# Moving one step of a gate's first layer, a residual and a variance bank in a two-block convolution kernel

## The chip, the cores and the metric

One Trainium2 chip, one of its cores. The metric is the device time of one execution in microseconds (us), taken as the median of several runs.

## What is computed

The input is `x` of shape (8, 64, 32, 32). Two blocks follow one another.

The first is a window attention block over channels: layer norm, attention in 8x8 windows with 8 heads and a relative bias, a projection and a residual, then layer norm, an MLP with GELU (64 to 256 to 64) and a second residual.

The second block, cut to what matters here:

```
h     = pw1 @ x + b                       # 1x1 convolution, 64 -> 64
score = sigmoid(fc2 @ relu(fc1 @ mean(h)))     # one per image and channel
mask  = the 32 largest scores of each image
off   = tanh(off_w @ mean(relu(h)))            # 3 x 2 per image
for ksz in (3, 5, 7):                          # depthwise, 32 channels
    w = base[ksz] * (1 + sigmoid(off[i, 0])) + tanh(off[i, 1])
    y[ksz] = dwconv(relu(h) * mask, w)
out = pw @ concat(y) + b + x
```

So each image has its own convolution weights, and they depend on the means of all its pixels. The chain from the means to the weights of an image is called its gate here.

## The kernel before, in words

Two images lie beside each other on the 128 partitions (`bh` is 0 or 1, 64 channels each), and four such pairs (`b4` is 0 to 3) follow in the free dimension: 4096 columns, worked on in 8 chunks of 512 columns (`NG` is 8).

**Attention.** A software pipeline over the 8 chunks: in the step of chunk g TensorE also does work of chunks g+1, g+2 and g-1. The second layer norm of a chunk is `centered2` (mean away), `variance2` (mean of squares), `inverse_deviation2` on ScalarE (Ln, then Exp), and `normalise2` on VectorE.

**MLP and pointwise stage.** For each chunk n: `mlp1(n)` makes four blocks of hidden values in PSUM banks 3 to 6, ScalarE's `gelu` empties them, `mlp2(n)` contracts them into bank 1, VectorE's `add_mlp(n)` adds them to x, `pointwise1(n)` makes h in bank 7 (even n) or 2 (odd n), ScalarE's `relu(n)` writes it into padded images, VectorE's `pool_image(n)` sums it, and GpSimd's `low_image(n)` makes its low part. The last chunk's second layer norm is still under way when this stage begins, so `variance2(7)` stands between `mlp2(1)` and `pointwise1(0)`. ScalarE loads the table for Ln and Exp ahead of `inverse_deviation2(7)` and the GELU table behind it.

**Gates.** Three gates: gate 0 for the pair b4=0, gate 1 for b4=1, gate 2 for b4=2 and 3. Each runs through `gate_means` (VectorE, then two matmuls on TensorE), `gate_hidden` (VectorE), `gate_scores` (TensorE, VectorE), `gate_spread` (VectorE, then two matmuls on TensorE), `gate_mask` and `gate_taps` (VectorE), and then for each image `products`, `add_products` (together `whole_weights`, VectorE) make the fp32 weights. Those are split into a high and a low part: ScalarE's `even_high` and `odd_row_weights` make the high part, VectorE's `low_even` and `low_odd` the low one.

**Convolution.** For each image, a unit (b4, bh): SP copies the padded image, shifted by 0 to 3 rows, onto the four groups of 32 partitions (`copy_images`, four transfers), and TensorE runs 14 tiles of taps. `high_passes` is 14 x 2 matmuls (high weights by high and low image), `low_passes` is 14 matmuls (low weights by high image): 42 matmuls of 512 columns per unit, 8 units. The matmuls of a unit add up in bank 3 + bh. VectorE's `result(b4, bh)` adds bias and residual, and SP stores the image. SP copies the images of the pair b4+1 once the unit (b4, bh) has ended.

**What sets the order.** Every engine's queue is written out by hand; each step waits on semaphores of the others. TensorE's order from the last MLP chunk on is: `pointwise1(5)`, `gate_means(1)`, `mlp2(6)`, `pointwise1(6)`, `gate_scores(1)`, `mlp2(7)`, then the units, with `gate_spread(1)`, `pointwise1(7)`, `gate_means(2)`, `gate_scores(2)` and `gate_spread(2)` put between passes. The lines of this part: L713 layer norm matmuls, L928 `mlp1`, L940 `mlp2`, L950 `pointwise1`, L956/L957 `gate_means`, L963 `gate_scores`, L970/L971 `gate_spread`, L1014 all convolution passes; VectorE L1155 `add_mlp`, L1229 `pool_image`, L1259 `gate_hidden`, L1265 `gate_scores`, L1275 to L1282 `gate_spread`, L1326 to L1337 `whole_weights`, L285 a low part, L1362 `result`; ScalarE L629 `gelu`, L638/L639 `relu`, L560/L564 Ln and Exp, L656/L271/L273 high weights; GpSimd L456 `low_image`; SP L382 `copy_images`, L386 store.

Of the kernel before, what the change touches and what calls it, by code (L numbers as in the profile page):

```python
# [12 lines left out]
NG = COLS // G  # L13
# [5 lines left out]
TAP = 7  # L19
# [7 lines left out]
NKT = (TAP + 1) // SHIFTS * TAP  # L27
# [71 lines left out]
def conv_seq_kernel(nc, d, out):  # L99
# [4 lines left out]
    with ctx:  # L104
# [116 lines left out]

        psum = ctx.enter_context(nc.psum_tensor("psum", [128, 8, 512], F32))
        NORM, MISC0, MISC1, MAX0, PROB0, PV = 0, 1, 2, 3, 5, 7
        VAR2_LAST = 6

        S = {n: sem(n) for n in (
            "zeroed", "k_heads_zeroed", "v_zeroed", "eps_set", "center_in", "consts_in", "x_first", "x_in0", "x_in1", "x_in2", "x_in3", "qkv_in", "raw_in", "weights_in", "rel_in",
# [10 lines left out]
        HIDDEN0, MLP, PW1, GATE, CONV0 = 3, 1, (7, 2), 0, 3  # L238
# [14 lines left out]
        def taps_window(w, m):  # L253

            o = (TAP - KERNELS[m]) // 2
            return w.rearrange("p (h x) o -> p h x o", x=TAP)[:, :, o:TAP - o, :]
# [26 lines left out]
        def low_part(engine, whole, high, low):  # L283

            return engine.tensor_tensor(low, whole, high.bitcast(F32), ALU.subtract)  # L285
# [188 lines left out]
        def _(act):  # L474
# [83 lines left out]
            def inverse_deviation2(c):  # L558
                act.wait_ge(S["pe_var2"], c + 1)
                act.activation(logvar2, psum[:, VAR2_LAST if isinstance(c, int) and c == NG - 1 else MISC0, :], ACT.Ln, bias=eps[:, 0:1]).then_inc(S["ac_log2"], 1)  # L560
                act.wait_ge(S["ac_log2"], c + 1)
# [147 lines left out]
        def _(pe):  # L709
            def over_channels(bank, which):  # L710

                for part in range(2):
                    ins = pe.matmul(psum[:, bank, :], center_average[:, which, :], parts[:, part, :], start=part == 0, stop=part == 1)  # L713
                return ins
# [110 lines left out]
            def variance2(c):  # L825
                pe.wait_ge(S["square2_low"], c + 1)
                bank = MISC0
                if isinstance(c, int) and c == NG - 1:
                    pe.wait_ge(S["ac_gelu"], 12)
                    bank = VAR2_LAST  # L830
                elif isinstance(c, int) and c + 3 >= NG:
                    pe.wait_ge(S["dv_q_low"], NG)
                    pe.wait_ge(S["ac_log2"], c)
                else:
                    pe.wait_ge(S["ac_log"], c + 4)
                over_channels(bank, 1).then_inc(S["pe_var2"], 1)
# [81 lines left out]
            def mlp1(n, blocks=range(4)):  # L918
                pe.wait_ge(S["dv_normed2"], 2 * n + 2)
                for m in blocks:  # L920
                    bh, f = m // 2, m % 2
                    if n > 0:
                        pe.wait_ge(S["ac_gelu"], 4 * n + m - 3)
                    if n == 3 and HIDDEN0 + m == VAR2_LAST:
                        pe.wait_ge(S["ac_log2"], NG)

                    for part in range(2):
                        ins = pe.matmul(psum[:, HIDDEN0 + m, :], mlp1_w[:, part, f * 128:(f + 1) * 128],  # L928
                                        normed2[:, bh, bass.ds(n * G, G)], start=part == 0, stop=part == 1)
                    ins.then_inc(S["pe_mlp1"], 1)  # L930
# [13 lines left out]
            def pointwise1(n, half):  # L944

                pe.wait_ge(S["dv_x2"], n + 1)
                if n > 1:
                    pe.wait_ge(S["ac_relu"], n - 1)
                    pe.wait_ge(S["dv_hsum"], n - 1)
                pe.matmul(psum[:, PW1[half], :], pw1_w, x2[:, bass.ds(n * G, G)], start=True, stop=True).then_inc(S["pe_pw1"], 1)  # L950
# [14 lines left out]
            def gate_spread(k):  # L965

                mem, n = gates[k], 2 * GATES[k][1]
                a = _AT["batch_of_row"][0]
                pe.wait_ge(S["gate_dve"], k * GATE_STEPS + 11)
                pe.matmul(psum[:, GATE, 128:128 + n * C], ones[0:n, :], mem["diag"][0:n], start=True, stop=True)  # L970
                pe.matmul(psum[:, GATE, 0:n], mem["score_rep"][0:n], consts[0:n, a:a + n], start=True, stop=True).then_inc(S["gate_pe"], 1)  # L971
# [36 lines left out]
            def passes(bh, w_part, tiles):  # L1008

                for t in tiles:  # L1010
                    y, x0 = t // TAP * SHIFTS, t % TAP
                    for part in range(2 - w_part):
                        img = shifted[:, bh, part, :].rearrange("p (y x) -> p y x", x=PW)
                        ins = pe.matmul(psum[:, CONV0 + bh, :], conv_w[bh][:, w_part, t, :], img[:, y:y + H - 1:2, x0:x0 + W],  # L1014
                                        start=t == 0 and w_part + part == 0, stop=t == NKT - 1 and w_part == 1)
                return ins

            def high_passes(b4, bh, tiles=range(NKT)):
                u = 2 * b4 + bh
                if tiles[0] == 0:  # L1020
                    pe.wait_ge(S["po_no_row"], bh + 1)
                    pe.wait_ge(S["ac_odd_high"], u + 1)
                    pe.wait_ge(S[f"shift_in{bh}"], 16 * SHIFTS * (b4 + 1))
                    if not (isinstance(b4, int) and b4 == 0):
                        pe.wait_ge(S["dv_result"], u - 1)
                passes(bh, 0, tiles)

            def low_passes(b4, bh):
                u = 2 * b4 + bh
                if not (isinstance(b4, int) and u == 0):  # L1030
                    pe.wait_ge(S["ac_odd"], u)
                pe.wait_ge(S["dv_odd"], u + 1)
                passes(bh, 1, range(NKT)).then_inc(S["pe_conv"], 1)
# [8 lines left out]
            high_passes(0, 1, range(TAP, NKT))  # L1042
            gate_scores(2)
            low_passes(0, 1)
            high_passes(1, 0, range(0, TAP))
            gate_spread(2)
            high_passes(1, 0, range(TAP, NKT))
            low_passes(1, 0)
            high_passes(1, 1)
            low_passes(1, 1)  # L1050
# [7 lines left out]
        def _(dve):  # L1058
# [197 lines left out]
            def gate_hidden(k):  # L1256
                mem, n = gates[k], 2 * GATES[k][1]
                dve.wait_ge(S["gate_pe"], k * GATE_PE + 1)
                dve.tensor_scalar(mem["fc1_out"], psum[:, GATE, 0:n], vec[:, 13:14], 0.0, ALU.add, ALU.max).then_inc(S["gate_dve"], 1)  # L1259
# [65 lines left out]
            def products(b4, bh):  # L1325
                dve.tensor_tensor(taps_window(whole_w[:, bh], 2), *factors(b4, bh, 2), ALU.mult)  # L1326
                dve.tensor_tensor(product5[:], *factors(b4, bh, 1), ALU.mult)
                dve.tensor_tensor(product3[:], *factors(b4, bh, 0), ALU.mult).then_inc(S["dv_product"], 1)

            def add_products(b4, bh):  # L1330
                u = 2 * b4 + bh
                dve.wait_ge(S["dv_product"], 2 * u + 1)
                window = taps_window(whole_w[:, bh], 1)
                dve.tensor_tensor(window, window, product5[:], ALU.add).then_inc(S["dv_product"], 1)
                dve.wait_ge(S["dv_product"], 2 * u + 2)
                window = taps_window(whole_w[:, bh], 0)
                dve.tensor_tensor(window, window, product3[:], ALU.add).then_inc(S["dv_whole"], 1)  # L1337

            def whole_weights(b4, bh):
                products(b4, bh)  # L1340
                add_products(b4, bh)

            def low_even(b4, bh):
                dve.wait_ge(S["ac_high"], 2 * b4 + bh + 1)
                low_part(dve, whole_w[:, bh], conv_w[bh][:, 0, :, 0:C], conv_w[bh][:, 1, :, 0:C]).then_inc(S["low_weights"], 1)
# [5 lines left out]
            def low_weights(b4, bh):  # L1351
                low_even(b4, bh)
                low_odd(b4, bh)

            def result(b4, bh):
                dve.wait_ge(S["pe_conv"], 2 * b4 + bh + 1)
                r = slice(bh * C, (bh + 1) * C)
                image = x2[r, bass.ds(b4 * PIX, PIX)].rearrange("p (y two x) -> p y two x", two=2, x=W)
                for parity in range(2):
                    rows = image[:, :, parity, :]  # L1360
                    made = psum[parity * C:(parity + 1) * C, CONV0 + bh, :].rearrange("p (y x) -> p y x", x=W)
                    ins = dve.scalar_tensor_tensor(rows, made, vec[parity * C:(parity + 1) * C, 10:11], rows, ALU.add, ALU.add)  # L1362
                ins.then_inc(S["dv_result"], 1)
# [21 lines left out]
            pool_image(4, 2, 0)  # L1385
            gate_means(1)
            products(0, 1)
            low_even(0, 0)
            add_mlp(6)
            gate_hidden(1)  # L1390
            add_products(0, 1)
            pool_image(5, 2, 1)
            gate_scores(1)
# [7 lines left out]
            pool_image(7, 3, 1)  # L1401
            gate_means(2)
            whole_weights(1, 0)
            result(0, 0)
            low_weights(1, 0)
            gate_hidden(2)
            whole_weights(1, 1)
            gate_scores(2)
            gate_spread(2)
# [87 lines left out]
```

## Time and profile before

| what | value |
|---|---|
| median of 3 runs | 355.97 us (354.71 to 358.31) |
| the profiled execution's own time | 358.61 us |
| its span in the profile | 356.8 us |
| busy in the span: TensorE matmul | 327.7 us (92%) |
| VectorE | 232.1 us (65%) |
| ScalarE | 206.1 us (58%) |
| GpSimd | 63.6 us (18%) |

The page divides the span into 40 slices of 8.92 us and gives each engine's busy share in tenths and TensorE's granted clock in tenths of full speed. The attention ends at about 213 us, the MLP and pointwise stage runs to 260 us, and the convolution from there to 352 us. Times in the rows count from the start of the span.

### The profile page before, as it was taken

What the parts mean: (1) busy time and instruction counts of PE and PEld (TensorE: products, weight loads), DVE (VectorE), ACT (ScalarE), POOL (GpSimd) and SP (SyncE); (2) the same over time, 40 slices, a digit from 0 to 9 for tenths busy, and PEclk for the clock granted to TensorE, in tenths of its full rate; (3) what the DMA queues carried; (4) which work ended last, traced back from release to release, by engine and by line L of the source; (5) the groups of instructions that cost most, each with busy time, mean ns of one, the idle gap of its engine ahead of it and who ended that gap; (6) DMA issues with size and microseconds to landing.
All of it is one profiled execution on the core that took longest, in us unless ns stands there. A gap on an engine that the chain in (4) does not pass through costs nothing.

```text
span 356.8 us, 6320 instructions
## 1 busy us (share of the span) xinstructions
PE 327.7 (92%) x2442; PEld 225.5 (63%) x2442; DVE 232.1 (65%) x403; ACT 206.1 (58%) x349; POOL 63.6 (18%) x58
## 2 busy tenths in 40 slices
PE   2668899999999999999998999699799899999994
PEld 2344675776767767677677765344367577777773
DVE  6566148188485693875847644578999989667411
ACT  6352835747568476585554468797891674445600
POOL 5461101211213212132011070122220000000000
PEclk9986999999999999999999999999999899999998
DMA  7533272322322133212232000058002665779721
GB/s 179 127 66 74 79 137 60 70 45 57 68 57 54 44 69 67 56 51 61 58 75 56 24 2 2 0 119 188 0 3 57 125 131 120 150 149 182 156 55 29
DMA packets 31148, 27.66 MB, mean 78 GB/s; under 512 B 21008, under 2 KB 27664, under 8 KB 31120
## 3 DMA queue, kind: packets, MB, share of 16 engines
q1 hardware_dynamic: 30544, 26.48, 35.3%
q10 hardware_dynamic: 576, 0.79, 0.9%
q8 instruction: 19, 0.31, 0.4%
q14 instruction: 9, 0.07, 0.1%
HBM read 3.78 MB, written 2.10 MB: 16 GB/s over the span
## 4 chain that ended last, share of the span: by engine, by line
PE 73%; DVE 12%; ACT 7%; DMA 3%; SPq 2%; issue 2%; POOL 1%; DVEq 0%; ACTq 0%
PE psum L1014 19%; PE psum L781 12%; PE psum L797 5%; PE psum L762 4%; PE psum L713 4%; PE psum L806 4%; PE psum L783 4%; PE psum L784 4%; PE psum L763 4%; PE psum L928 3%; DVE maxima L1123 3%; PE psum L740 2%; DMA probs<-in_rel_table 2%; PE psum L814 2%; PE psum L940 2%
## 5 line engine op out<-in xcount | busy, mean ns | idle before, releaser
L1014 PE MATMUL psum<-shifted,conv_w 128*128 128x512 f32 x336 | 87.9, 424 | 0.0
L1014 PEld LDWEIGHTS psum<-shifted,conv_w 128*128 128x128 f32 x336 | 65.0, 194 | 21.8 <-issue 1.3
L543 ACT ACTIVATE probs<-psum 128x512 f32<-128x512 f32 x64 | 38.3, 599 | 50.2 <-PE psum L784 49.3
L781 PE MATMUL psum<-q_heads,k_blocks 128*128 128x512 f32 x192 | 59.7, 419 | 0.0
L1123 DVE TENSOR_REDUCE maxima<-psum 128x8 f32<-128x512 f32 x64 | 41.2, 685 | 23.9 <-PE psum L763 23.9
L781 PEld LDWEIGHTS psum<-q_heads,k_blocks 128*128 128x128 f32 x192 | 35.0, 189 | 14.2 <-issue 7.7
L285 POOL TENSOR_TENSOR parts<-x,parts 128x256 fp32r<-128x256 f32 (+1 forms) x21 | 19.1, 922 | 101.8 <-ACT parts L492 56.9
L762 PE MATMUL psum<-k_heads,q_blocks 128*128 128x512 f32 x64 | 27.8, 434 | 4.0 <-DMA k_heads<-k_parts 3.4
L713 PE MATMUL psum<-parts,center_average 128*128 128x512 f32 x64 | 22.4, 434 | 9.6 <-DVE parts L285 7.9
L1137 DVE RECIPROCAL inv_sum<-psum 128x256 f32<-128x256 f32 x16 | 28.0, 1750 | 3.3 <-PE psum L806 3.2
L271 ACT CAST conv_w<-conv_w 32x896 fp32r<-32x896 f32 x31 | 29.1, 938 | 0.4
L1362 DVE SCALAR_TENSOR_TENSOR x<-psum,weights,x 64x512 f32<-64x512 f32 x16 | 12.0, 749 | 24.9 <-PE psum L1014 24.8
L285 POOL TENSOR_TENSOR parts<-square_logvar,parts 128x512 fp32r<-128x512 f32 x14 | 18.1, 1291 | 55.5 <-ACT square_logvar L498 27.9
L763 PE MATMUL psum<-rel,reverse 128*128 128x512 f32 x64 | 26.5, 414 | 0.0
L656 ACT CAST conv_w<-whole_w 128x896 fp32r<-128x896 f32 x8 | 7.5, 939 | 31.4 <-DVE whole_w L1337 16.6
L783 PE MATMUL psum<-rel,reverse 128*128 128x512 f32 x64 | 25.1, 393 | 0.0
L784 PE MATMUL psum<-minus_max,pick 128*128 128x512 f32 x64 | 25.0, 391 | 0.0
L713 PEld LDWEIGHTS psum<-parts,center_average 128*128 128x128 f32 x64 | 12.0, 202 | 14.5 <-issue 6.8
L629 ACT ACTIVATE hidden<-psum,mlp_bias 128x512 f32<-128x512 f32 x32 | 19.6, 701 | 2.6 <-PE psum L928 2.6
L928 PE MATMUL psum<-normed,mlp_w 128*128 128x512 f32 x64 | 18.3, 423 | 2.7 <-ACT square_logvar L560 2.2
L797 PEld LDWEIGHTS psum<-probs,v_blocks 128*32 128x32 f32 x1024 | 15.0, 110 | 8.0 <-issue 8.0
L762 PEld LDWEIGHTS psum<-k_heads,q_blocks 128*128 128x128 f32 x64 | 12.9, 202 | 11.0 <-issue 6.7
(142 smaller groups left out, 506.3 us busy)
## 6 DMA issues: line engine op xcount, KB each, us to landing
shifted<-images SPq DMA_DIRECT2D x32, 332.5 KB, 5.5
k_blocks<-k_parts SPq DMA_DIRECT2D x32, 128.0 KB, 2.8
q_heads<-q_parts SPq DMA_DIRECT2D x128, 32.0 KB, 1.9
k_heads<-k_parts SPq DMA_DIRECT2D x64, 32.0 KB, 1.8
out<-x SPq DMA_DIRECT2D x8, 256.0 KB, 5.5
x<-in_x SPq DMA_DIRECT2D x6, 256.0 KB, 5.0
x<-in_x SPq DMA_DIRECT2D x4, 128.0 KB, 4.4
weights<-in_weights ACTq DMA_DIRECT2D x1, 443.0 KB, 7.6
```

The costliest lines, as they stand in the source:

```text
L271: ins = copy(conv_w[bh][shift * KS:(shift + 1) * KS, part, :, C:], w[(shift - 1) * KS:shift * KS, :, 0:C])
L285: return engine.tensor_tensor(low, whole, high.bitcast(F32), ALU.subtract)
L543: act.activation(probs[:, w, :], psum[:, PROB0 + w % 2, :], ACT.Exp).then_inc(S["ac_probs"], 1)
L713: ins = pe.matmul(psum[:, bank, :], center_average[:, which, :], parts[:, part, :], start=part == 0, stop=part == 1)
L762: pe.matmul(max_bank(w), q_blocks[:, w, :], k_heads[:, :, w * T:(w + 1) * T], start=True, stop=False)
L763: pe.matmul(max_bank(w), reverse[:], rel[:, 0, :], start=False, stop=True).then_inc(S["pe_max"], 1)
L781: pe.matmul(bank, k_blocks[:, w // (NW // 2), k_part, w % (NW // 2), :], q_heads[:, q_part, :, w * T:(w + 1) * T], start=k_part + q_part = ...
L783: pe.matmul(bank, reverse[:], rel[:, 1, :], start=False, stop=False)
L784: pe.matmul(bank, pick[:, w, :], minus_max[:, :, :], start=False, stop=True).then_inc(S["pe_scores"], 1)
L797: pe.matmul(psum[32 * j:32 * j + 32, PV, p * T:(p + 1) * T], v_blocks[:, par, at:at + 32], probs[:, w, head * T:(head + 1) * T], start=hh ...
L1014: ins = pe.matmul(psum[:, CONV0 + bh, :], conv_w[bh][:, w_part, t, :], img[:, y:y + H - 1:2, x0:x0 + W], start=t == 0 and w_part + part == ...
L1123: dve.tensor_reduce(maxima[:, w * NH:(w + 1) * NH], max_bank(w).rearrange("p (h t) -> p h t", t=T), AX.X, ALU.max).then_inc(S["dv_max"], 1)
```

## The change

Three steps change their place in an engine's order (on TensorE `gate_spread(2)`, on VectorE `low_even(0, 0)` and `gate_hidden(2)`), and one variance its PSUM bank, with the waits that guard it. No instruction is added or taken away.

```
-        VAR2_LAST = 6
+        VAR2_LAST = 2
...
 def variance2(c):        # TensorE
                 if isinstance(c, int) and c == NG - 1:
-                    pe.wait_ge(S["ac_gelu"], 12)
+                    pe.wait_ge(S["ac_proj"], NG)
                     bank = VAR2_LAST
...
 def mlp1(n, blocks):     # TensorE
-                    if n == 3 and HIDDEN0 + m == VAR2_LAST:
-                        pe.wait_ge(S["ac_log2"], NG)
...
 def pointwise1(n, half): # TensorE
                 pe.wait_ge(S["dv_x2"], n + 1)
+                if n == 1:
+                    pe.wait_ge(S["ac_log2"], NG)
...
 # TensorE's order
             low_passes(0, 1)
-            high_passes(1, 0, range(0, TAP))
+            high_passes(1, 0)
             gate_spread(2)
-            high_passes(1, 0, range(TAP, NKT))
             low_passes(1, 0)
...
 # VectorE's order
             products(0, 1)
-            low_even(0, 0)
             add_mlp(6)
             gate_hidden(1)
+            low_even(0, 0)
             add_products(0, 1)
...
             gate_means(2)
             whole_weights(1, 0)
+            gate_hidden(2)
             result(0, 0)
             low_weights(1, 0)
-            gate_hidden(2)
             whole_weights(1, 1)
```

The variance of the last chunk goes to bank 2, which held the last projection, and bank 2 is the one that `pointwise1(1)` writes next; before it went to bank 6, which held the last hidden block of chunk 2 and would hold that of chunk 3.

## Rows read from the trace of the kernel before

**Rows 1.** The page, part 4: shares of the chain that ended last, by engine.

```profile
PE 73%; DVE 12%; ACT 7%; DMA 3%; SPq 2%; issue 2%; POOL 1%; DVEq 0%; ACTq 0%
```

**Rows 2.** Waits of TensorE, 225 to 357 us: waiter <- awaited: total us, times, longest.

```profile
PE psum L928 <- ACT square_logvar L560: 2.2, 1, 2.2
```

**Rows 3.** Timeline, 223 to 234 us: start, duration, engine, line, operation, idle before.

```profile
223.10 1.27 ACT L629 ACTIVATE hidden<-psum,mlp_bias 128x512 f32<-128x512 f32 x2
223.25 0.69 DVE L285 TENSOR_TENSOR parts<-square_logvar,parts 128x512 fp32r<-128x512 f32 x1 [2.29 <-ACT square_logvar L556]
...
224.51 0.71 PE L713 MATMUL psum<-parts,center_average 128*128 128x512 f32 x2 [0.56 <-ACT hidden L629]
...
226.12 0.69 ACT L638 ACTIVATE square_logvar<-psum,weights 128x512 f32<-128x512 f32 x1 [1.75 <-PE psum L950]
...
233.56 2.37 PE L928 MATMUL psum<-normed,mlp_w 128*128 128x512 f32 x8 [0.49 <-ACT hidden L629]
```

**Rows 4.** Timeline, 255 to 261 us, as rows 3.

```profile
255.19 1.08 DVE L285 TENSOR_TENSOR conv_w<-whole_w,conv_w 128x896 fp32r<-128x896 f32 x1
...
256.19 0.74 DVE L1155 SCALAR_TENSOR_TENSOR x<-psum,weights,x 128x512 f32<-128x512 f32 x1
...
256.61 1.19 POOL L456 TENSOR_TENSOR images<-square_logvar,images 128x512 fp32r<-128x512 f32 x1 [6.13 <-ACT images L639]
...
256.98 1.50 DVE L1334 TENSOR_TENSOR whole_w<-whole_w,product 128x640 f32<-128x640 f32 x1
...
256.99 1.13 PE L950 MATMUL psum<-x,weights 128*128 128x512 f32 x2 [1.39 <-DVE x L1155]
257.13 1.88 ACT L271 CAST conv_w<-conv_w 32x896 fp32r<-32x896 f32 x2
...
260.12 3.81 PE L1014 MATMUL psum<-shifted,conv_w 128*128 128x512 f32 x14
```

**Rows 5.** VectorE's line L1334: min/median/max ns, first and last start.

```profile
L1334 DVE TENSOR_TENSOR whole_w<-whole_w,product x8: 824/825/1501, 248.5 to 326.4; 128x640 f32<-128x640 f32 x8
```

**Rows 6.** Timeline, 276 to 291 us.

```profile
276.32 3.79 PE L1014 MATMUL psum<-shifted,conv_w 128*128 128x512 f32 x14
277.17 0.56 DVE L1337 TENSOR_TENSOR whole_w<-whole_w,product 128x384 f32<-128x384 f32 x1
...
281.60 0.22 DVE L1259 TENSOR_SCALAR gate_memory<-psum,weights 128x4 f32<-128x4 f32 x1
...
281.88 0.28 PE L963 MATMUL psum<-weights,gate_memory 128*4 128x64 f32 x2 [1.76 <-DVE gate_memory L1259]
...
282.08 8.74 PE L1014 MATMUL psum<-shifted,conv_w 128*128 128x512 f32 x28
```

**Rows 7.** TensorE alone by windows: busy us (instructions), granted clock, DMA share, GB/s.

```profile
227.47:231.10 3.63, 1.46 (x4) 1.00 0.00 0
279.60:283.00 3.40, 1.64 (x9) 1.00 0.73 151
283.05:286.46 3.41, 3.41 (x10) 0.50 0.02 5
```

**Rows 8.** Groups of TensorE, 291.49 to 352 us: busy us, mean ns, idle before.

```profile
L1014 PE MATMUL psum<-shifted,conv_w 128*128 128x512 f32 x238 | 60.4, 417 | 0.0
```

**Rows 9.** Timeline of VectorE, ScalarE and SP, 262 to 299 us.

```profile
262.15 0.27 DVE L1282 TENSOR_TENSOR gate_memory<-gate_memory,consts 2x128 f32<-2x128 f32 x1
...
272.79 4.16 SPq L382 DMA_DIRECT2D shifted<-images  x4
...
279.31 2.83 ACT L271 CAST conv_w<-conv_w 32x896 fp32r<-32x896 f32 x3
...
286.52 0.41 DVE L1282 TENSOR_TENSOR gate_memory<-gate_memory,consts 4x256 f32<-4x256 f32 x1
...
298.52 0.56 DVE L1337 TENSOR_TENSOR whole_w<-whole_w,product 128x384 f32<-128x384 f32 x1
```

**Rows 10.** The transfers of `copy_images`: us from issue to landing.

```profile
DMA to landing us min/median/max: 3.4/5.5/6.4
```

More of the change, by code:

```diff
@@ L223, in conv_seq_kernel @@
         NORM, MISC0, MISC1, MAX0, PROB0, PV = 0, 1, 2, 3, 5, 7
-        VAR2_LAST = 6
+        VAR2_LAST = 2
         S = {n: sem(n) for n in (
@@ L828, in variance2 @@
                 if isinstance(c, int) and c == NG - 1:
-                    pe.wait_ge(S["ac_gelu"], 12)
+                    pe.wait_ge(S["ac_proj"], NG)
                     bank = VAR2_LAST
@@ L923, in mlp1 @@
                         pe.wait_ge(S["ac_gelu"], 4 * n + m - 3)
-                    if n == 3 and HIDDEN0 + m == VAR2_LAST:
-                        pe.wait_ge(S["ac_log2"], NG)
                     for part in range(2):
@@ L946, in pointwise1 @@
                 pe.wait_ge(S["dv_x2"], n + 1)
+                if n == 1:
+                    pe.wait_ge(S["ac_log2"], NG)
                 if n > 1:
@@ L1044, in _ @@
             low_passes(0, 1)
-            high_passes(1, 0, range(0, TAP))
+            high_passes(1, 0)
             gate_spread(2)
-            high_passes(1, 0, range(TAP, NKT))
             low_passes(1, 0)
@@ L1387, in _ @@
             products(0, 1)
-            low_even(0, 0)
             add_mlp(6)
             gate_hidden(1)
+            low_even(0, 0)
             add_products(0, 1)
@@ L1403, in _ @@
             whole_weights(1, 0)
+            gate_hidden(2)
             result(0, 0)
             low_weights(1, 0)
-            gate_hidden(2)
             whole_weights(1, 1)
```

## The prediction

> **What bounds the kernel now.** I read the chain that ended last first: 73% of the span is TensorE and 12% VectorE [rows 1]. So TensorE's gaps and what fills them come next. From 291.49 us to the end 238 convolution matmuls take 60.4 us, 0.254 us each, with no idle ahead of them [rows 8]; nothing can be won there by order. What is left are the places ahead of that where TensorE stands still. Its waits and its timeline show four between 223 and 283 us: 0.56 us at 224.51 for a GELU, 2.2 us at 229.64 for the last Ln [rows 2, 3], 1.39 us at 256.99 for the residual `add_mlp(6)` [rows 4], and 1.76 us at 281.88 for `gate_hidden(2)` [rows 6]. Behind the last one the granted clock is 0.50, the lower of TensorE's two levels (1.2 GHz), from 283.05 to 286.46 us [rows 7]. The change touches all four.
>
> **The bank of the last variance.** At 224.51 TensorE starts `variance2(7)`, because bank 6 is free only when the second pair of GELUs ends at 223.10 + 1.27 = 224.37. Its data, VectorE's low part, is there at 223.25 + 0.69 = 223.94, and TensorE is free at 224.51 - 0.56 = 223.95 [rows 3]. In bank 2 the wait is for a projection evacuated long before. With the same 0.14 us from release to start it begins at 224.08: 0.43 us earlier. ScalarE waited 1.75 us for the following `pointwise1(0)` until 226.12, and from there it works through (relu, tables, Ln, Exp, relu, GELUs) until it releases TensorE at 233.56 [rows 3]. So the 0.43 us passes through. The 2.2 us wait does not vanish: the same Ln now holds `pointwise1(1)` in place of the last block of `mlp1(3)`, whose two matmuls move ahead of the wait. That moves TensorE's slack and nothing of ScalarE's chain, so I cost it at nothing; if ScalarE were not the cover, it would be worth the two matmuls, about 0.5 us more. **Term: 0.43 us**, between 0.3 (release later than I take) and 0.56.
>
> **The residual ahead of the low part.** VectorE runs the low part for 1.08 us from 255.19, then `add_mlp(6)` from 256.19, and only its end lets `pointwise1(6)` start at 256.99; the matmuls of `mlp2(6)` had ended at 256.99 - 1.39 = 255.60 [rows 4]. With the low part behind, the residual starts at about 255.64 and takes 0.74: TensorE idles 0.04 + 0.74 + 0.05 = 0.83 in place of 1.39. **Term: 0.56 us.** It passes to the convolution's start at 260.12 if the high weights of unit (0,0) are there. ScalarE ends them at 257.13 + 1.88 = 259.01 [rows 4], now 258.58 with the first term; TensorE comes at 260.12 - 0.99 = 259.13. Margin 0.55 us.
>
> What the low part does in its new place is open. VectorE loses the 0.4 us that it now waits for `mlp2(6)`, and the low part meets GpSimd's `low_image(5)` (256.61 for 1.19 us [rows 4]; some 0.4 us earlier after the change). An operation of this kind, two inputs in SBUF, does suffer there: L1334 at 256.98 took 1.50 us and its median is 0.825 [rows 4, 5]. So VectorE already pays 0.68 us for this collision, and after the change either the low part or the two sums behind it pay; the bounds are nothing more and 1.19 us more. The first TensorE wait that this could lengthen is `gate_spread(1)`, which stands behind 14 matmuls of the first unit: TensorE comes to it at 260.12 + 3.75 - 0.99 = 262.9 us, and VectorE is done at 262.15 + 0.27 = 262.42 [rows 4, 9]. Part of this lateness is swallowed again, so I take nothing; the upper bound costs up to 0.7 us there. The Trainium skill ("SBUF — State Buffer", section "SBUF: two separate sides") says that of such a VectorE operation and a GpSimd one, whichever starts first holds the shared port pair for its whole length and the other blocks; the 0.68 us of the row agrees, and the rule makes the outcome hang on which starts first.
>
> **The hidden layer of the third gate ahead of the first result.** TensorE ends the passes before it at 276.32 + 3.79 = 280.11 and waits until 281.88 because on VectorE `gate_hidden(2)` (281.60) comes after `result(0,0)` and the low weights. Its input is ready much earlier, and `whole_weights(1,0)` ends at 277.17 + 0.56 = 277.73 [rows 6]; right behind it the 0.22 us operation ends near 277.95, ahead of TensorE's new time 280.11 - 0.99 = 279.12. **Term: 1.76 us.** What moves behind it (the first result, its store, the low weights) is 0.2 us later and is needed only from low passes (1,0) on, over 8 us later.
>
> **The clock.** The 28 matmuls from 282.08 take 8.74 us [rows 6]; at the 0.254 us of rows 8 they would take 7.10. The clock falls after a stretch with 1.64 us busy in 3.40, and in this stretch lies the stall that goes [rows 7]. **Term: 1.64 us**, bounds 0 and 1.64. The trace also shows that a gap alone doesn't decide: behind the 2.2 us wait the clock stayed at 1.00 [rows 2, 7]. So in some executions the stall costs its 1.76 us only. The Trainium skill ("TensorE: Matmul & The Clock Gate", section "What's actually happening") says that the chip's observation is free-running and does not restart with a kernel, which fits that a larger gap went unpunished; by it the term changes from execution to execution.
>
> **The third gate's spread behind all high passes.** It costs the same 0.7 us of TensorE in either place. TensorE now comes to low passes (0,1) at 279.3, to high passes (1,0) at about 283.0, and to the spread at 283.0 + 7.4 = 290.4. VectorE has finished its part at 286.52 + 0.41 = 286.93 [rows 9]. Had it stayed in the middle, TensorE would have come at 286.7, so the move covers this wait. Late next is VectorE's mask behind the spread: it starts near 291.2, as before, since TensorE's gain is spent on the 14 matmuls in front. The weights of (2,0) that follow it are whole at 298.52 + 0.56 = 299.1 [rows 9] or a little earlier, and ScalarE needs for their high part what it needs for that of (1,0), 282.14 - 277.73 = 4.4 us, so 303.5; TensorE comes at 291.2 + 42 x 0.254 + 14 x 0.254 = 305.4. Margin 1.9 us, so the move costs nothing.
>
> Other margins: high weights of (1,0) end at 279.31 + 2.83 = 282.14 [rows 9], or 281.7 with the first term, against 283.0. Their image copies are issued from 272.79 for 4.16 us and land within 6.4 us [rows 9, 10]: 282.4 at the latest if the last is issued at 276.0, and 281.4 after the change, since the unit that releases them ends 0.99 us earlier.
>
> **The sum.** 0.43 + 0.56 + 1.76 + 1.64 = 4.39 us from the profiled execution's 358.61, which gives 354.2. That execution lies 2.6 us above the median of the runs, and whether the median run had the fall of the clock is not shown. For the median I weigh the clock term by 0.6: 0.43 + 0.56 + 1.76 + 1.0 = 3.75, so **352.2 us** (355.97 - 3.75), with its own range 351.0 to 353.3.
>
> **Rivals.**
> A: The early terms are lost. VectorE comes late to `gate_spread(1)` or ScalarE to the first high weights, whose margins are the smallest; only the stall goes and part of the clock: 355.97 - 1.76 - 0.6 = 353.6. For it speak the collision and the 0.4 us that VectorE now waits, against it that a later GpSimd collision absorbed such lateness.
> B: The clock. It falls at another place, or the median run had no fall: 355.97 - 2.75 = 353.2; with one more fall of 1.64 us inside the convolution, 354.9. For it speaks that TensorE's gap near 229 stays, against it that this gap left the clock alone here.
> C: The change does not do what it says for the third gate: TensorE waits the same time at high passes (1,0), for ScalarE's high weights (282.14), because the margin of 1.3 us is used up by VectorE's delays. Up to 1.3 us back: 355.97 - 2.4 = 353.5.
> D: Slower. The image copies of (1,0) and (1,1) now have 11.3 and 11.9 us between release and use, where (1,0) had 13.4. If their landing took not 6.4 but 12.8 us under the denser traffic, each would come at 3.2 + 12.8 = 16.0 and TensorE would wait 4.7 and 4.1 us: 355.97 - 3.75 + 8.8 = 361.0. It decides from 8.1 us of landing on. Against it: later units work at 42 x 0.254 = 10.7 us of distance without idle [rows 8] and no landing exceeds 6.4 us [rows 10].
>
> **Chances.** Forecast 0.50, A 0.14, B 0.22, C 0.08, D 0.03, and 0.03 for a small loss of another kind. The range holds the forecast's own range, A, B's and C's: 350.8 to 354.9. A difference of 1% (3.56 us) is about what a measurement tells from none. The forecast lies just beyond it, so it splits: faster by over 1% 0.50 (of the forecast 0.38, of B and the runs' own spread 0.12), within 1% 0.46, slower 0.04.
>
> **What would show it.** In the changed kernel's profile: `variance2(7)` idles under 0.2 us and the Ln is 0.4 us earlier; L950 for chunk 6 idles 0.8 us; the convolution starts at 259.1; L963 for the third gate has no idle ahead; the granted clock stays at 1.00 from 276 to 292; L970 with 4x256 has no idle. Wrong would be a new wait of TensorE at L1014 or L970, naming DVE, ACT or DMA, or a fall of the clock elsewhere after 240 us.

## The result

The changed kernel takes 353.74 us (median of 4 runs, 353.00 to 354.98) where the kernel before takes 357.14 us (4 runs, 354.71 to 359.16): a ratio of 0.9899, 95% interval 0.9851 to 0.9947. Timed again, as `after_again` below, it is 353.92 to 357.92 us and 0.9887 (0.985 to 0.9924). The forecast was 352.2 us, that is 3.75 us less than the 355.97 us then known; measured are 3.4 us between the medians and 3.6 to 4.0 us by the two ratios. The 353.74 us lie in the stated range (350.8 to 354.9) but above the forecast's own (351.0 to 353.3), because the kernel before was 1.2 us slower in these four runs than the 355.97 us that were subtracted from. Both ratios lie just beyond 1%, and both intervals reach to either side of it. Of the 25 runs of the kernel before that the first four experiments are compared with, one took 632.66 us and is left out. The profiled executions are 358.61 before and 354.98 after.

The page of the changed kernel: busy time of TensorE, granted clock by slices, and the shares of the chain that ended last.

```profile
PE 325.4 (92%) x2442; PEld 223.8 (63%) x2442; DVE 234.1 (66%) x403; ACT 206.0 (58%) x349; POOL 64.1 (18%) x58
...
PEclk9986899999999999999999999999999999999998
...
PE 82%; DVE 9%; ACT 4%; issue 2%; SPq 1%; POOL 1%; DMA 1%; DVEq 0%; ACTq 0%
```

The chain is now 82% TensorE where it was 73% [rows 1], and 9% VectorE where it was 12%. In the clock line the 8 that stood in slice 32 of the kernel before (276 to 285 us) is a 9. The waits of TensorE from 222 us on (waiter <- awaited: total us, times, longest):

```profile
PE psum L950 <- ACT square_logvar L560: 1.7, 1, 1.7
PE psum L926 <- ACT hidden L629: 1.0, 1, 1.0
PE psum L950 <- DVE x L1154: 0.9, 1, 0.9
PE psum L956 <- DVE gate_memory L1252: 0.4, 1, 0.4
```

The wait for `gate_hidden(2)` is no longer there, and the one for the Ln has another waiter, `pointwise1(1)`, and 1.69 us in place of 2.17. Its row before, the last two matmuls of `mlp1(3)`:

```profile
229.64 0.70 PE L928 MATMUL psum<-normed,mlp_w 128*128 128x512 f32 x2 [2.17 <-ACT square_logvar L560]
```

Now the same stretches of the timeline as before the prediction (start, duration, engine, line, operation, idle before). First 223 to 234 us; this execution is 0.6 us later than the other when the last chunk's layer norm begins, from its attention stage, so intervals are compared and not starts.

```profile
223.85 0.69 DVE L285 TENSOR_TENSOR parts<-square_logvar,parts 128x512 fp32r<-128x512 f32 x1 [2.29 <-ACT square_logvar L556]
...
224.60 0.74 PE L713 MATMUL psum<-parts,center_average 128*128 128x512 f32 x2
...
226.23 0.69 ACT L638 ACTIVATE square_logvar<-psum,weights 128x512 f32<-128x512 f32 x1 [1.25 <-PE psum L950]
...
233.67 2.37 PE L926 MATMUL psum<-normed,mlp_w 128*128 128x512 f32 x8 [0.95 <-ACT hidden L629]
```

From the low part's start to `variance2(7)` are 224.60 - 223.85 = 0.75 us, before 224.51 - 223.25 = 1.26 [rows 3]: 0.51 us gained. From there to the first `mlp1(4)` are 9.07 us, before 9.05: ScalarE's chain passes it on unchanged. TensorE waits 0.95 us there in place of 0.49, since its two matmuls are already done.

```profile
255.76 0.75 DVE L1154 SCALAR_TENSOR_TENSOR x<-psum,weights,x 128x512 f32<-128x512 f32 x1 [0.37 <-PE psum L938]
...
256.56 1.08 DVE L285 TENSOR_TENSOR conv_w<-whole_w,conv_w 128x896 fp32r<-128x896 f32 x1
...
256.57 1.12 PE L950 MATMUL psum<-x,weights 128*128 128x512 f32 x2 [0.85 <-DVE x L1154]
...
256.73 1.97 POOL L456 TENSOR_TENSOR images<-square_logvar,images 128x512 fp32r<-128x512 f32 x1 [6.14 <-ACT images L639]
257.25 1.89 ACT L271 CAST conv_w<-conv_w 32x896 fp32r<-32x896 f32 x2
257.56 1.82 DVE L1333 TENSOR_TENSOR whole_w<-whole_w,product 128x640 f32<-128x640 f32 x1
...
259.70 3.80 PE L1014 MATMUL psum<-shifted,conv_w 128*128 128x512 f32 x14
```

Here `pointwise1(6)` waits 0.85 us in place of 1.39, and from `variance2(7)` to the convolution are 35.10 us in place of 35.61. GpSimd's `low_image(5)` takes 1.97 us in place of 1.19, and L1333 (L1334 before) 1.82 in place of 1.50 [rows 4].

```profile
262.38 0.27 DVE L1281 TENSOR_TENSOR gate_memory<-gate_memory,consts 2x128 f32<-2x128 f32 x1
...
277.87 0.21 DVE L1258 TENSOR_SCALAR gate_memory<-psum,weights 128x4 f32<-128x4 f32 x1
...
279.54 2.84 ACT L271 CAST conv_w<-conv_w 32x896 fp32r<-32x896 f32 x3
...
279.62 0.28 PE L963 MATMUL psum<-weights,gate_memory 128*4 128x64 f32 x2
...
279.82 10.89 PE L1014 MATMUL psum<-shifted,conv_w 128*128 128x512 f32 x42
...
286.87 0.41 DVE L1281 TENSOR_TENSOR gate_memory<-gate_memory,consts 4x256 f32<-4x256 f32 x1
...
290.64 0.69 PE L970 MATMUL psum<-gate_memory,small 4*128 4x256 f32 x2
```

`gate_hidden(2)` is done at 278.08 us, TensorE needs it at 279.62 and does not stand still. 42 matmuls now take 10.89 us at full clock, 0.26 us each, where the 28 of before took 8.74, 0.31 us each [rows 6] (windows of TensorE alone: busy us, instructions, granted clock, DMA share, GB/s; compare [rows 7]):

```profile
279.60:283.00 3.40, 3.40 (x16) 1.00 0.59 126
283.05:286.46 3.41, 3.41 (x15) 1.00 0.48 102
```

```profile
L1014 PE MATMUL psum<-shifted,conv_w 128*128 128x512 f32 x224 | 56.9, 418 | 0.0
```

The rest of the convolution, 224 matmuls in 56.9 us, runs at 0.254 us each as before [rows 8]. VectorE's last `result` starts at 351.96 us before and at 348.31 now. From the start of the low part (223.25 and 223.85) these are 128.71 us before and 124.46 after: 4.25 us less over the same work. The profiled times differ by 3.63 only, because of the 0.6 us at the start.

### The profile page after: what moved, and what is told of

It is laid out like the page before. It is cut to its first block, busy times and chain, and to the rows that moved or that the text cites. A ratio compares the mean times of both kernels' runs of the same rounds, so it can differ in the third digit from the quotient of the medians.

```text
span 353.2 us, 6320 instructions
## 1 busy us (share of the span) xinstructions
PE 325.4 (92%) x2442; PEld 223.8 (63%) x2442; DVE 234.1 (66%) x403; ACT 206.0 (58%) x349; POOL 64.1 (18%) x58
## 4 chain that ended last, share of the span: by engine, by line
PE 82%; DVE 9%; ACT 4%; issue 2%; SPq 1%; POOL 1%; DMA 1%; DVEq 0%; ACTq 0%
PE psum L1014 24%; PE psum L781 12%; PE psum L797 5%; PE psum L713 4%; PE psum L762 4%; PE psum L806 4%; PE psum L783 4%; PE psum L784 4%; PE psum L763 4%; PE psum L938 3%; PE psum L926 3%; DVE maxima L1122 3%; PE psum L740 2%; PE psum L814 2%; PE psum L745 2%
## 5 line engine op out<-in xcount | busy, mean ns | idle before, releaser
L1014 PE MATMUL psum<-shifted,conv_w 128*128 128x512 f32 x336 | 86.5, 419 | 0.0
L1014 PEld LDWEIGHTS psum<-shifted,conv_w 128*128 128x128 f32 x336 | 63.9, 191 | 21.6 <-issue 1.3
L713 PEld LDWEIGHTS psum<-parts,center_average 128*128 128x128 f32 x64 | 11.9, 200 | 15.6 <-issue 8.4
```

## Experiments

Theory: the gain is the sum of the 0.5 us of the bank, the 0.5 us of the residual, the 1.76 us of the stall, and a fall of the clock that the stall brings. Rivals: the early terms are lost, or the fall has another cause. Each kernel is timed beside the kernel before; the first four on one chip, the last four on another.

**The bank alone** (`bank_alone`): the kernel before with

```
-        VAR2_LAST = 6
+        VAR2_LAST = 2
```

and the waits that go with it.

> Only the last variance goes to bank 2; the residual, the hidden layer and the spread of the third gate stay. If the terms add up one by one: the 0.56 us idle of TensorE ahead of variance2(7) goes, GELUs of chunk 3 and all behind come 0.4 to 0.55 us earlier, the stall ahead of the third gate's scores stays at about 1.8 us because VectorE, which sets its end, comes earlier by the same amount; total gain 0.4 to 0.55 us, not to be told from nothing by the times. If the Ln wait, which now holds pointwise1(1), eats it: the GELUs of chunk 3 start no earlier against variance2(7) and the gain is 0. Clock: the stall of 1.8 us is there, so a fall behind it is expected unless the stall is cut in two by the chip's observation.

Ratio 0.9991 (0.9954 to 1.0029). The stall's row and the window behind it:

```profile
279.36 0.28 PE L963 MATMUL psum<-weights,gate_memory 128*4 128x64 f32 x2 [1.76 <-DVE gate_memory L1259]
```

```profile
280.60:284.00 3.40, 3.40 (x9) 0.50 0.02 5
```

The stall is 1.76 us, the same; the clock falls behind it. In this trace `variance2(7)` starts 2.53 us after the matmuls of `centered2(7)` (221.97 and 219.44), before 3.04 (224.51 and 221.47), and the convolution starts 35.63 us behind it, before 35.61. So the 0.51 us gets through to the convolution in the profile, and as the stall keeps its length it gets past the scores too; the times can't resolve it.

**The residual alone** (`residual_alone`):

```
             products(0, 1)
-            low_even(0, 0)
             add_mlp(6)
             gate_hidden(1)
+            low_even(0, 0)
```

> Only the low part goes behind add_mlp(6) and gate_hidden(1). Adding-up theory: the idle ahead of pointwise1(6) falls from 1.39 to 0.85 us and the convolution starts 0.5 us earlier, but the end of the stall ahead of the third gate's scores is set by VectorE, which does not come earlier: the stall grows from 1.76 to 2.2 to 2.4 us and the total gain is about 0. So this edit is worth nothing without the hidden layer's move. Rival: the gain of 0.5 us passes to the end, stall 1.76 us as before. A clock fall of 3.41 us behind the stall is expected in both.

Ratio 0.9986 (0.9955 to 1.0016). The stall's row, and the window behind it:

```profile
280.98 0.28 PE L963 MATMUL psum<-weights,gate_memory 128*4 128x64 f32 x2 [2.41 <-DVE gate_memory L1259]
```

```profile
282.60:286.00 3.40, 3.40 (x10) 0.51 0.02 5
```

This stretch takes in a little of the full clock ahead of the fall, hence the 0.51. The convolution starts 35.07 us behind `variance2(7)` (258.58 and 223.51), 0.54 less than before, and the stall is 2.41 us in place of 1.76. As the theory said: VectorE sets the stall's end, and what TensorE gains ahead of it is given back there. So by itself the edit brings nothing; with the hidden layer's move its 0.5 us is kept (what the whole change has over `hidden_alone` is put into figures under `after_again`).

**The hidden layer alone** (`hidden_alone`):

```
             whole_weights(1, 0)
+            gate_hidden(2)
             result(0, 0)
             low_weights(1, 0)
-            gate_hidden(2)
```

> Only gate_hidden(2) goes ahead of result(0,0); the spread stays in the middle of high passes (1,0). Theory: stall of 1.76 us gone, and with it the fall of the clock behind it: L1014 between 280 and 291 us at 0.254 to 0.266 us a matmul, gain 1.76 us plus up to 1.64 us, 3.4 us in a profile where before falls. TensorE comes to the spread at about 287.5 us, VectorE has its input ready at 286.9: no wait or under 0.2 us. Rival (the fall has another cause): clock falls near 283 to 286 all the same, gain 1.76 us.

Ratio 0.9895 (0.9851 to 0.9939), 354.68 us. TensorE's rows from the scores on, and the windows ahead of and in its one fall of the clock outside the attention's start:

```profile
279.60 0.27 PE L963 MATMUL psum<-weights,gate_memory 128*4 128x64 f32 x2
279.81 7.36 PE L1014 MATMUL psum<-shifted,conv_w 128*128 128x512 f32 x28
```

```profile
226.00:229.60 3.60, 1.43 (x5) 1.00 0.00 0
229.60:233.00 3.40, 3.40 (x9) 0.50 0.00 0
```

No idle at L963, and the 28 matmuls take 7.36 us in place of 8.74: by the rows this single move brings about 3.1 us where the clock would fall, 1.76 for the stall and 1.38 for the clock; the ratio says 3.8 us (2.2 to 5.3), and doesn't tell this kernel from the whole change. The clock fell elsewhere in this execution, behind the wait for the Ln, at 229.6 us. The way from `variance2(7)` to the convolution was 36.42 us there (223.25 to 259.67), 0.81 more than before: in this one execution a fall in the ScalarE-bound stage cost a little over half of the 1.38 us among back-to-back matmuls.

**The stall filled** (`fill_stall`): the order of the kernel before, and ahead of the third gate's scores

```
             high_passes(0, 1, range(TAP, NKT))
+            for t in range(6):
+                img = shifted[:, 1, 0, :].rearrange("p (y x) -> p y x", x=PW)
+                pe.matmul(psum[:, 5, :], conv_w[1][:, 0, t, :], img[:, 0:H - 1:2, 0:W], start=True, stop=True)
             gate_scores(2)
```

> The order is that of the kernel before; TensorE only does six more matmuls of 128x512 (into the unused bank 5, read by nobody) where it stood still ahead of the third gate's scores. They take 6 x 0.254 = 1.5 us of the 1.76 us stall. If the idle time causes the fall of the clock: clock 1.00 from 276 to 292, the 28 matmuls behind take 7.1 to 7.4 us in place of 8.74, and the kernel is up to 1.6 us faster although it does more work and the third gate's hidden layer comes no earlier. If the fall has another cause (the engine's load, the transfers beside it): clock 0.50 for 3.4 us all the same and no gain.

Ratio 0.9951 (0.9926 to 0.9975), 356.32 us: 0.9 to 2.6 us faster with six matmuls more. The added ones (L1045), what is left of the stall, and the 28 matmuls behind:

```profile
280.02 1.61 PE L1045 MATMUL psum<-shifted,conv_w 128*128 128x512 f32 x6
281.94 0.28 PE L963 MATMUL psum<-weights,gate_memory 128*4 128x64 f32 x2 [0.30 <-DVE gate_memory L1262]
282.14 7.35 PE L1014 MATMUL psum<-shifted,conv_w 128*128 128x512 f32 x28
```

```profile
280.20:281.94 1.74, 1.44 (x7) 1.00 0.97 199
281.94:289.42 7.48, 7.48 (x30) 1.00 0.33 69
```

The third gate's hidden layer came no earlier. The 28 matmuls take 7.35 us as in `hidden_alone`, and the clock stays at 1.00. So the idle time causes the fall at this place; the fall alone costs 1.4 us by the rows and 1.75 us by the ratio.

**The changed kernel again** (`after_again`), unaltered.

> The changed kernel unaltered, beside the kernel before on one chip. Theory (three stalls and one fall of the clock): ratio 0.987 to 0.990, and no fall of the clock between 270 and 300 us. If the clock fall were a matter of one execution only, the ratio would be 0.992 to 0.994.

Ratio 0.9887 (0.985 to 0.9924). No fall after 29.3 us in its profile. Each run also states its mean granted clock; with two levels, twice (1 - clock) times the span is the time at the lower one. It is 11.9 us on average over the 24 runs before of the first chip that the comparison uses (0.977 to 0.990) and 12.0 over the 16 of the second, 8.6 over the 10 runs of the changed kernel (0.983 to 0.993), and 7.5 over the 10 of `fill_stall`. Over all kernels run here it is 11.7 us with the stall (60 runs, four sets) and 8.1 us without it or with it filled (43 runs). The difference is 3.6 us (95% interval 2.4 to 4.7), one fall as long as the 3.41 us in [rows 7]; no run with the stall has under 6 us at the lower level, and 13 of the 43 others have. So on average the stall brought one whole fall, not 0.6 of one.

The same figures explain most of the spread of the times. The profiles have further falls at the start of the attention, all before 40 us: 3.4 us at the lower level in `bank_alone`, `residual_alone`, `hidden_alone` and `after_again`, 6.8 in `after_spread_back` and `vector_late`, and 10.2 in the other four; what remains of a run's figure, up to 3 us, lies at the very end, behind the last matmul. Within the runs of one kernel the time rises by 0.31 us for each us at the lower level (103 runs in 11 sets, correlation 0.88), 1.0 us for a fall of 3.41. An estimate follows from this: taken at equal time at the lower level, each beside its own runs of before, `bank_alone` is 0.3 us faster (-0.2 to 0.7), `residual_alone` 0.0 (-0.4 to 0.5), `fill_stall` 0.1 (-0.4 to 0.5), `hidden_alone` 1.7 (1.3 to 2.0) and the changed kernel 2.8 (2.6 to 3.0). It prices every fall alike, which for one fall among the matmuls (0.40 us for each us, 1.38 in 3.41) is 0.3 us too little. The gain of `fill_stall` is thus the clock's alone, and the whole change has 1.1 us (0.7 to 1.5) more than the hidden layer's move by itself: the 1.0 us of the bank and the residual.

**The spread put back** (`after_spread_back`): the changed kernel with

```
-            high_passes(1, 0)
+            high_passes(1, 0, range(0, TAP))
             gate_spread(2)
+            high_passes(1, 0, range(TAP, NKT))
```

> The changed kernel with gate_spread(2) put back into the middle of high passes (1,0). TensorE comes there at 287.15 us, and in the changed kernel VectorE has the input ready at 287.28: a wait of 0.1 to 0.3 us, and the mask and the weights of (2,0) come some 3.3 us earlier, which nobody needs. So this part of the change is worth 0.1 to 0.3 us, and not to be told by the times. Rival (the move is what makes the hidden layer's move pay): a wait of over 1 us at L970 and a ratio clearly above the changed kernel's.

Ratio 0.9865 (0.9822 to 0.9908), not to be told from `after_again`.

```profile
286.03 0.69 PE L970 MATMUL psum<-gate_memory,small 4*128 4x256 f32 x2 [0.15 <-DVE gate_memory L1282]
```

The wait is 0.15 us. The move of the spread is worth that much and costs nothing.

**VectorE made late** (`vector_late`): the changed kernel with

```
             gate_means(2)
+            for bank in (5, 6, 7):
+                dve.tensor_tensor(psum[:, bank, :], weights[:, 0:512], weights[:, 0:512], ALU.mult)
             whole_weights(1, 0)
             gate_hidden(2)
```

> The changed kernel with three more VectorE operations of 128x512 (into PSUM banks read by nobody, some 2.0 us in all) ahead of whole_weights(1,0), to see how thick the cover is that the change leans on. In the changed kernel the high weights of (1,0) end at 282.4 us and TensorE begins with them at about 283.5: 1.1 us of cover. Theory: TensorE waits 0.3 us at the third gate's scores and about 0.5 to 0.7 us at high passes (1,0), 0.9 us in all, far less than the 2.0 us added. If VectorE were what bounds the start of the convolution, the whole 2.0 us would show.

Ratio 0.9906 (0.9876 to 0.9935). The added work, the scores and the first passes of (1,0):

```profile
272.98 1.90 DVE L1403 TENSOR_TENSOR psum<-weights 128x512 f32<-128x512 f32 x3
...
278.71 0.28 PE L963 MATMUL psum<-weights,gate_memory 128*4 128x64 f32 x2 [0.26 <-DVE gate_memory L1258]
...
283.04 7.31 PE L1014 MATMUL psum<-shifted,conv_w 128*128 128x512 f32 x28 [0.32 <-issue]
```

From the convolution's start to the third gate's spread are 31.83 us (258.45 to 290.28), in `after_again` 30.95 (258.11 to 289.06): 0.88 us for 1.8 us of added work (the next operation starts at 274.78), 0.34 of it ahead of the scores and 0.54 behind. The expectation of 0.9 holds. The cover behind the changed order is thus about 1 us thick, in one profile.

**Tables first** (`tables_first`): the changed kernel with, on ScalarE,

```
-            relu(0, 0, 0)
             load_tables(LN_AND_EXP)
             inverse_deviation2(NG - 1)
             load_tables(GELU)
+            relu(0, 0, 0)
             relu(1, 0, 1)
```

and on VectorE `pool_image(0)` behind `normalise2(7)` and its split.

> The changed kernel with one more edit: ScalarE's two table loads, Ln and Exp of the last variance go ahead of relu(0) in place of behind it, and on VectorE normalise2(7) with its split goes ahead of pool_image(0). ScalarE idled 1.25 us for pointwise1(0) there. Theory (ScalarE's chain from the last variance to the first GELU of chunk 3 sets the stage): the GELUs of chunk 3 start 1.2 us earlier than in the changed kernel, TensorE's wait for the last Ln (1.7 us) falls under 0.2 us, and the kernel is 1.1 to 1.3 us faster than the changed one. Rival (VectorE's pool_image and gate_means(0) set the stage): the 1.2 us are gone before the convolution starts and the time stays.

353.05 us, ratio 0.9848 (0.9809 to 0.9887), beside 0.9887 for the changed kernel on the same chip. The intervals overlap; taken at equal time at the lower level, as above, it is 1.4 us faster than the changed kernel (0.7 to 2.0, an estimate). The profile: ScalarE from the last GELU of chunk 2 on, and TensorE's wait for chunk 3's.

```profile
223.99 1.27 ACT L629 ACTIVATE hidden<-psum,mlp_bias 128x512 f32<-128x512 f32 x2
...
225.28 1.28 ACT L480 ACT_TABLE_LOAD   x1
...
226.58 0.69 ACT L560 ACTIVATE square_logvar<-psum,eps 128x512 f32<-128x512 f32 x1
...
229.25 0.69 ACT L638 ACTIVATE square_logvar<-psum,weights 128x512 f32<-128x512 f32 x1
...
232.58 2.37 PE L926 MATMUL psum<-normed,mlp_w 128*128 128x512 f32 x8 [1.51 <-ACT hidden L629]
```

ScalarE no longer idles for `pointwise1(0)`, TensorE no longer waits for the Ln, and from `variance2(7)` (224.89) to the convolution (258.61) are 33.72 us, in `after_again` 35.07 (223.04 to 258.11): 1.35 us less, as the expectation's first theory says. TensorE's wait for a GELU ahead of `mlp1(4)` is longer, 1.51 us in place of 0.95: ScalarE still bounds this stage. This version has the lowest median of those run here.

## Why the prediction was right, step by step

- **The bank.** Forecast 0.43 us, measured 0.51. I took 0.14 us from release to start; it was 224.60 - 224.54 = 0.06. That ScalarE's chain passes it on held (9.07 and 9.05 us), and so did the slack: the Ln wait moved to `pointwise1(1)`.
- **The residual.** Forecast 0.56 us, idle down to 0.83; measured 0.54 and 0.85 by the waits, and 0.51 from `variance2(7)` to the convolution. The high weights ended at 257.25 + 1.89 = 259.14 against a start at 259.70: margin 0.56, forecast 0.55.
- **The collision with GpSimd.** I left it open within 1.19 us. The low part started at 256.56, ahead of `low_image(5)` at 256.73; GpSimd then took 0.78 us more and L1333 0.32 us more. The trace agrees with the Trainium skill's rule ("SBUF — State Buffer", section "SBUF: two separate sides") that whichever starts first holds the pair: had GpSimd waited for the low part's end at 257.64 and then taken its 1.19 us, it would have ended at 258.83, and it ended at 258.70. TensorE felt none of it: VectorE's input for `gate_spread(1)` was ready at 262.65, TensorE came at 263.43.
- **The stall.** Forecast and measured 1.76 us of idle; from the convolution's start to the scores are 21.76 us before and 19.92 after, 1.84 less.
- **The clock.** Forecast 1.64 us where it falls; by the rows 8.74 - 7.36 = 1.38. I priced the 28 matmuls at 28 x 0.254 = 7.10 us. But a row runs to the end of its last matmul, and a group's last one takes 0.43 us until the next work starts, not 0.254: in `hidden_alone` the 28 take 7.29 us from their start to that of the spread (279.81 to 287.10), 27 x 0.254 + 0.43. The 8.74 holds that too, so 0.26 us of the 1.64 was never the clock's. For the median I weighed the term by 0.6, because a gap of 2.2 us had gone unpunished. That was the weakest step: the clocks of the runs say that on average one whole fall came with the stall. The two errors pull against each other: 1.0 stood in the sum where about 1.4 belongs, and that the total came out so near owes something to luck.
- **The sum** in the profiled execution, forecast 4.39: by stretches of the two traces, 0.51 us are gained up to `variance2(7)`, 0.51 from there to the convolution, 1.84 from there to the scores and 1.39 from there to the last result, 4.25 in all. The waits and the matmuls' row alone add up to 0.51 + 0.54 + 1.76 + 1.38 = 4.19.
- **The spread** costs nothing, and the mask's chain met TensorE with time to spare: no wait at (2,0).
- **The rivals.** A (early terms lost) fell: both terms reached the convolution. What `residual_alone` adds is that the residual's term is there only because the stall is gone, a dependence that the prediction didn't name. B (another fall) is what single executions show (`hidden_alone` at 229.6), not what the median shows. C and D did not come: the high weights of (1,0) were ready at 279.54 + 2.84 = 282.38 against about 283.5, and no transfer is among TensorE's waits.
- **What stays open.** The medians differ by 3.4 us and the ratios say 3.6 and 4.0, where the sum over the same work says 4.25. The ratios' intervals (1.9 to 5.3 us for the first) hold them all, and the falls at the start of the attention, 3.4 to 10.2 us at the lower level in one profile or another, shift a median of four runs by a microsecond. At equal time at the lower level the changed kernel is 2.8 us faster, where the stretches without the clock give 0.51 + 0.51 + 1.84 = 2.86; one fall adds 1.0 to 1.4. Why the number of those early falls changes from run to run, and why the gap at the Ln brought a fall once only, no run here shows.

## What to carry to other kernels

A stall among back-to-back matmuls can cost its length and then again what the clock takes back, so it is worth more than the wait list says; and the place of the stall matters, for a fall cost 0.8 us in a stage bound by another engine (one profile) and 1.4 us among the matmuls. Where runs differ in how long the clock was low, compare them at equal time at the lower level before reading a small difference of medians. Gains ahead of a wait that another engine ends are lost at that wait: remove the last wait too, then the earlier gains add up. To find out what a stall costs beyond its length, fill it with useless matmuls and time that.

## What the runs showed of the hardware

- Six useless matmuls in a 1.76 us gap made the kernel faster by 0.5% (0.25% to 0.74%). Behind the unfilled gap, 1.76 us in the kernel before and `bank_alone` and 2.41 us in `residual_alone`, the granted clock was 0.50 for 3.4 us in all three profiles; in the seven profiles with the gap gone or filled it was 1.00 there.
- The wait for the Ln, 2.17 us, brought a fall in one profile (`hidden_alone`) and none in three (the kernel before, `residual_alone`, `fill_stall`), with the same instructions up to there. The length of a gap alone does not decide it.
- A fall of 3.41 us cost 1.38 us among back-to-back matmuls, 0.81 us in the stage bound by ScalarE, and about 1.0 us on average over falls at any place (0.31 us for each us at the lower level).
- The collision of VectorE and GpSimd goes both ways: GpSimd's operation took 1.97 us in place of 1.19 when the VectorE operation had started 0.17 us ahead of it.
